# Filler products taken off TensorE's first steps in a fused four-layer kernel

## The reference

```python
# layer 0: a grouped convolution over positions, then a base matrix and low-rank experts
out  = conv1d(x, weight, 9 taps, 4 groups) + (cond_128 @ c_weight.T)[:, :, None] + bias
base = out @ base_W.T
top2 = softmax(top_k(out @ gate_W.T, 2))
x    = x + base + sum_e top2[e] * 2 * (out @ lora_A[e].T) @ lora_B[e].T
# layers 1, 2, 3 begin with the same small network on cond_128 (three layers, 8 scores each)
h    = gelu(cond_128 @ W0 + b0);  h = gelu(h @ W1 + b1)
att  = softmax(h @ W2 + b2)
out  = einsum('boi,bih->boh', einsum('bk,koi->boi', att, weight), x) + (att @ bias_k)[:, :, None]
# their ffn: layer 1 an 8-bit quantised 512x512 product, layer 2 silu(gate) * up with 1792
# hidden columns and a product down, layer 3 two of three experts for each batch row
```

## Time and profile before

| | before |
|---|---|
| median of three runs | 740.83 us |
| the profiled execution's own time | 739.74 us |
| its span from the first to the last instruction | 737.9 us |
| TensorE busy | 726.4 us (98%) |
| VectorE busy | 460.0 us (62%) |
| ScalarE busy | 299.6 us (41%) |
| GpSimd busy | 344.1 us (47%) |
| mean granted TensorE clock | 1.000 |

### The profile page before, as it was taken

One profiled execution on the slowest core, in us unless ns is written; L12 is line 12 of the kernel. 1 busy time (PEld: TensorE's weight loads), 2 busy tenths in 40 slices (PEclk: granted clock), 3 DMA queues, 4 the chain that ended last, 5 costly groups with the idle time before them and its releaser, 6 DMA issues.

```text
span 737.9 us, 11037 instructions
## 1 busy us (share of the span) xinstructions
PE 726.4 (98%) x3550; PEld 591.0 (80%) x3566; DVE 460.0 (62%) x1060; ACT 299.6 (41%) x577; POOL 344.1 (47%) x386
## 2 busy tenths in 40 slices
PE   8899999999999999999999999999999999999997
PEld 5688777877788888888888888887788887888886
DVE  4977667778623345663467345887778887755533
ACT  5644445444432333254334334232554334534321
POOL 3656677676425522121221015867755545464630
PEclk9999999999999999999999999999999999999999
DMA  8666447544051122110220102514513211221200
GB/s 289 126 135 173 148 139 214 158 143 144 30 184 58 29 65 78 58 29 1 86 89 26 30 21 69 182 48 137 175 44 117 71 58 59 59 87 43 73 29 29
DMA packets 44775, 68.91 MB, mean 93 GB/s; under 512 B 21248, under 2 KB 21600, under 8 KB 44464
## 3 DMA queue, kind: packets, MB, share of 16 engines
q1 hardware_dynamic: 34816, 37.77, 16.9%
q0 software_dynamic: 9152, 29.69, 13.1%
q10 hardware_dynamic: 752, 0.74, 0.3%
HBM read 45.03 MB, written 17.65 MB: 85 GB/s over the span
## 4 chain that ended last, share of the span: by engine, by line
PE 83%; POOL 6%; DVE 4%; issue 3%; DMA 3%; ACT 1%; POOLq 0%; DVEq 0%; ACTq 0%
PE bank L2238 22%; PE bank L2217 13%; PE bank L2185 12%; PE bank L2090 10%; PE bank L1875 8%; PE bank L1806 4%; PE bank L1911 3%; PE bank L2196 2%; POOL wur L699 2%; DMA raw<-in_w_dram 2%; PE bank L1945 2%; PE bank L1923 1%; PE bank L2110 1%; PE bank L2047 1%; POOL wgr L697 1%
## 5 line engine op out<-in xcount | busy, mean ns | idle before, releaser
L1658 DVE TENSOR_TENSOR sil<-bank,sil 128x512 f32<-128x512 f32 x56 | 38.6, 689 | 93.2 <-PE bank L2238 93.2
L2238 PE MATMUL bank<-th,wur 128*128 128x512 f32 x224 | 87.8, 392 | 0.0
L2090 PE MATMUL bank<-wda,hh 128*128 128x512 f32 x224 | 87.5, 391 | 0.0
L2238 PE MATMUL bank<-tl,wur 128*128 128x512 f32 x224 | 87.2, 389 | 0.0
L2090 PE MATMUL bank<-wda,hl 128*128 128x512 f32 x224 | 87.2, 389 | 0.0
L2238 PE MATMUL bank<-th,wgr 128*128 128x512 f32 x224 | 87.2, 391 | 0.0
L2238 PE MATMUL bank<-tl,wgr 128*128 128x512 f32 x224 | 86.8, 390 | 0.0
L2185 PE MATMUL bank<-wda,xch 128*128 (+1 forms) x272 | 84.6, 392 | 0.1
L1113 ACT ACTIVATE hh<-sil 128x512 fp32r<-128x512 f32 x56 | 35.4, 632 | 117.0 <-DVE sil L1658 117.0
L1660 DVE TENSOR_TENSOR hl<-sil,hh 128x512 fp32r<-128x512 f32 x56 | 45.6, 814 | 39.1 <-ACT hh L1113 39.1
L1105 ACT ACTIVATE sil<-bank 128x512 f32<-128x512 f32 x56 | 33.4, 596 | 89.4 <-PE bank L2238 89.3
(11 more groups left out here) (365 smaller groups left out, 1778.6 us busy)
## 6 DMA issues: line engine op xcount, KB each, us to landing
tap<-in_x_taps_dram SPq DMA_DIRECT2D x16, 260.0 KB, 2.8
xin<-in_x_rows_dram SPq DMA_DIRECT2D x16, 256.0 KB, 3.0
xd<-xo SPq DMA_DIRECT2D x16, 256.0 KB, 3.2
xc<-xd SPq DMA_DIRECT2D x16, 256.0 KB, 4.6
xres<-xd SPq DMA_DIRECT2D x4, 1024.0 KB, 5.6
xd<-xres SPq DMA_DIRECT2D x4, 1024.0 KB, 5.0
tsd<-tf SPq DMA_DIRECT2D x4, 1024.0 KB, 4.2
raw<-in_w_dram POOLq DMA_DIRECT2D x16, 256.0 KB, 3.0
```

Of the source, the lines that this page charges most:

```text
L1658: v.tensor_tensor(hf[:, m % 2], p_pre[(2 * m + 1) % 3][:], sil[:, m % 2], ALU.mult).then_inc(s_hf, 1)
L2090: last = mm(p_acc[j][:], h[:, m % HSLOTS, j * P:(j + 1) * P], wda[:, m * D:(m + 1) * D], start=(m == 0 and n == 0), stop=(m == MT - 1 and ...
L2238: last = mm(p_pre[(2 * m + b) % 3][:], w[:, (m * KT + kt) * P:(m * KT + kt + 1) * P], x[:, kt], start=(kt == 0 and n == 0), stop=(kt == KT ...
```

## The change

All 25 filler products go, and with them the memset of `junk` and its semaphore. The tile `junk` itself stays, and so does the order of everything else.

```diff
@@ semaphores
-        s_const, s_junk = sem("s_const"), sem("s_junk")
+        s_const = sem("s_const")
@@ VectorE
-            v.memset(junk[:], 1.0).then_inc(s_junk, 1)
             v.memset(att3[:].bitcast(F32), 0.0)
@@ TensorE
-            def keep_busy(n):
-
-                for _ in range(n):
-                    mm(bank[3][:], junk[:].bitcast(BF16)[:, 0:P], junk[:].bitcast(BF16)[:, 0:512], start=True, stop=True)
-
-            pe.wait_ge(s_junk, 1)
-            keep_busy(14)
             pe.wait_ge(s_cvw, 2)
             conv(0)
@@ after the first layer of the small networks
-            keep_busy(4)
             pe.wait_ge(s_const, 9)
             positions(0)
@@ before the first router
             scores()
-            keep_busy(3)
             router(0)
```

## The result

The changed kernel takes 745.03 us in the median of 8 executions (742.31 to 745.54), the kernel before 740.85 us (8 executions). The ratio is 1.0043, with a 95% interval of 1.0029 to 1.0057: slower by 0.43%, some 3.2 us. The executions of the changed kernel fall into two heaps. Over all 20 that were timed, 6 have a mean granted clock of 0.999 or 1.000 and a median of 742.6 us, and 14 have 0.998 or less and a median of 745.1 us. Of 86 executions of the kernel before, 16 have 0.998 or less (median 743.4 us) and the others a median of 740.8 us.

A forecast was written before the change was run, and what follows sets the result against it. TensorE was taken as the bound, busy 726.4 of 737.9 us, with VectorE full to 38.7 us. The terms, 1.60 + 0.1 = +1.7 us, took the median from 740.83 to 742.5 us, range 741.3 to 745.0.

The forecast's parts named there:

- The memset and the first fourteen gain nothing: Before `conv(0)`: removing VectorE's 0.48 us memset and the fourteen products ending at 6.56 us gains 0; `conv(0)` waits for `cvl`.
- All nine products of `conv(0)` slow, +1.60: From 7.22 us: `conv(0)`'s nine products run at the low rate, 3.84 us in place of 2.24, so +1.60 us.
- +0.1 for line 1830, 0 for the small products: Behind `conv(0)`: line 1830's product, partly slow, costs +0.1 us; the small products after it cost 0.
- the likeliest case: About all of `conv(0)` slow and nothing behind it: +1.1 to +2.3 us, 741.9 to 743.1 us, chance 50%.
- 0 for the 4, 4 and 3: Later filler: two fours hidden by ScalarE, 0; the three before `router(0)` taken as 0, bounds 0 to -0.65 us.
- the late rise: Rival: rate stays low through small products, rising only after about 3.8 us of `router(0)` and `conv(1)`; +3.7 us, 744.5, 18%.
- TensorE's full list passes that on to the end.: After 38.7 us: TensorE has no room, so the start's delay reaches the end, +1.7 us.
- The gather's wait might take up 0.8: Rival, last phase: TensorE's 0.8 us gather wait absorbs delay, leaving 0.9 of 1.7, 741.7 us; 6% with no effect.

The follow-up runs named there:

- e2_small_gone: Kernel before without the later 4, 4 and 3 filler products, the first fourteen kept: 742.74 us, ratio 1.0013.
- e8_7_more_tiny: Kernel before plus seven filler products of 8 columns behind the first fourteen, where TensorE waits for `cvl` anyway: 742.67 us, ratio 1.0014.
- e5_perm_late: Kernel before with `permutation(0)` put one block of eight products later on TensorE: 741.01 us, ratio 1.0005.

## Why the prediction was right, and where it fell short

The direction, the likeliest mechanism and the range held (742.5 us, 741.3 to 745.0, slower 0.56). The size was about half of the measured one: 1.7 us against 3.2 by the ratio and 4.2 by the medians.

- *The memset and the first fourteen gain nothing.* Held: `conv(0)` starts at 7.17 against 7.22, still released by `cvl`.
- *All nine products of `conv(0)` slow, +1.60.* Held: 7.17 to 11.18 is 4.01 us against 2.24, so +1.77. The first spacing is 0.6 us, which the sum of nine equal ones left out.
- *+0.1 for line 1830, 0 for the small products.* Nearly: the scores are late by 1.92 in the one profile. `base(0)` is late by 1.83 in the other, hung on `w0l`, where the sum had 1.7; 0.20 of it is a `conv(0)` that could start only at 7.42 there. What I called the likeliest case is this one, and the executions whose clock stays up have a median of 742.6 us.
- *0 for the 4, 4 and 3.* This is the first term that was mis-sized. Their time is hidden, as costed; what they keep up isn't. I asked whether the clock would have risen by then, and gave the late rise 18%. It did rise and fell again at 16 us, after 4.5 us in which TensorE had only small products and pauses. By e2_small_gone that costs 1.0 us with a fast `conv(0)`, by the two profiles of the changed kernel 0.7 to 0.8. Of its 20 executions, 14 have a lowered clock, though the mean doesn't tell this fall from the one near 510 us. The rival had the right place (`router(0)` at 0.21 us a product, `base(0)` no longer released by `w0l`) and the wrong road to it.
- *"TensorE's full list passes that on to the end."* This is the step that failed. The delay itself is passed on unchanged: 2.66 at 21.56 us, 2.68 at 500 us. But the change took 50 instructions off TensorE's list, and with them moved its fetches. One had held up a load of GpSimd's weights in the kernel before, and thereby kept GpSimd out of VectorE's way during the tiny steps that make `hot`. By the runs with `permutation(0)` put later this makes 1.6 to 1.9 us of the loss, and by e8_7_more_tiny, which shifts no work, 1.0 by the ratio and 1.85 by the medians. I costed the products by their time and never by their number. The page of before even showed that there are fetches, 31 on queue 8, in a line that I passed over; after the change it has 30.
- *The gather's wait might take up 0.8.* It did in the profile (0.4 came back), but it isn't dependable: the kernel before has it at 0.8, 1.1 and 2.2 us in its three profiles.

That small steps of VectorE stretch to the end of a GpSimd instruction is read from the rows. In them the stretched steps have all their operands in SBUF and more than one of them, and those with one operand, or with one in a PSUM bank, aren't stretched; no run here varies that, so the reason stays open. That the fetch delays the load is shown by a tie and by the order of packets: five profiles in which the load's last packet comes behind a fetch and GpSimd waits, eight without either, and two kernels made to move the fetch that did as foretold. That fetch and last packet share one of the 16 DMA engines fits this order, but the trace doesn't name a packet's engine. Nor does it show why, in e5_perm_late, GpSimd went on only at 505.28, 1.2 us after that packet's start. That the fetches are TensorE's is argued from their moving with its list. Which part of the clock's fall at 16 us is due to the small products' width and which to the pauses wasn't tried.

## What to carry to other kernels

Filler on TensorE is worth what it keeps up, and that is read at the places where little else runs: ask of each piece which full-size products come next and at which of the two rates they would go, also when the first warm-up stays in place. Adding or removing instructions moves the fetches of everything behind them; when a difference appears hundreds of microseconds after an edit, compare the instruction queue with the loads there, and test with products that are as many but tiny. And take several profiles and the clock of each execution before a small difference is explained: here a single profile of before showed neither its own late executions nor that its luck near 504 us hung on a fetch.

## What the runs showed of the hardware that was not expected

- The granted clock column reads 1.00 up to its first recorded change: `conv(0)` ran with 0.43 us for 512 columns under a granted 1.00.
- The clock fell after waits of 1.7 us (before `hot`) and 2.2 us (for the gather) in otherwise dense work, and after 4.5 us of small products with pauses of 0.5 and 0.8 us. It doesn't in every execution: the profile of e8_7_more_tiny has waits of 1.7 and 1.9 us at a granted 1.00, and the second of the changed kernel has pauses of 1.0 and 0.8 us and then a fast `router(0)`.
- A VectorE instruction on 64x3 elements took 1.20 us beside a GpSimd tensor instruction, and 0.14 us without. One that read an operand from a PSUM bank took 0.15 us beside it.
- Where a 16 KB fetch of instructions, of 0.97 to 1.94 us, came ahead of a 256 KB load's last packet, GpSimd waited 1.2 to 1.6 us for the load; where the fetch fell between two loads it didn't wait.
- Two profiles of the same changed kernel differ in how long the low rate lasted: in the first all nine products of `conv(0)` were slow and the six records of line 1825 took 1.34 us; in the second the ninth product took 0.30 us to the next start in place of 0.43, and the six records 0.83 us. That agrees with the Trainium skill (TensorE: Matmul & The Clock Gate, Part 1), by which the number of slow products differs from run to run.
